# Scaling a gathered unit in three operations instead of one, in a deformable-convolution kernel

## The reference

```python
offset = conv3x3(x, w_off, b_off)              # two offsets for each of nine taps; C1 and C2 also a mask
py, px = row + tap_row + off_y, column + tap_column + off_x
for each of the four neighbours of (py, px):
    acc = acc + weight * valid * x[:, :, y_neighbour, x_neighbour]     # bilinear sample
out = einsum('bckhw,ock->bohw', acc * mask, w_dcn)
# batch norm, then relu (L0) or gelu (C1, C2); C2 also adds its block's input
```

## Time and profile before

| | |
|---|---|
| median of three runs | 10,226.54 us (10,207.91 to 10,236.34) |
| profiled execution, first to last instruction (span) | 7,289.1 us |
| profiled execution's own time | not shown apart; the runs' median less the span is 2,937.4 us |
| PE busy | 5,861.0 us, 80% |
| POOL busy | 5,125.5 us, 70% |
| DVE busy | 4,797.0 us, 66% |
| ACT busy | 2,151.4 us, 30% |
| gather issues on POOL | 4,896, 5,111.4 us, mean 1,044 ns |
| scale on DVE | 476 + 68, 647.2 + 92.3 us |

### The profile page before, as it was taken

The page is one execution under the profiler, slowest core; times in us unless marked ns, Lnnn a source line. Parts: engine busy times, 40 slices in busy tenths (PEclk is TensorE's granted clock), DMA queues, the critical chain, the costliest instruction groups (busy, mean ns, idle before and its releaser), DMA issues. The chain is left out here.

```text
span 7289.1 us, 123281 instructions
## 1 busy us (share of the span) xinstructions
PE 5861.0 (80%) x46325; PEld 4691.8 (64%) x46325; DVE 4797.0 (66%) x11223; ACT 2151.4 (30%) x3327; POOL 5125.5 (70%) x4909
## 2 busy tenths in 40 slices
PE   6985666664787887787887788879989998998996
PEld 6874555553666675576665565557767776776775
DVE  7875666664677775677775455546766766775665
ACT  1221212221222222222222222224444443443442
POOL 0007777777777776777776777767777777777776
PEclk9986777775888897788997788889989998998998
DMA  4322333333333332333332222223323333333332
GB/s 145 101 91 85 89 94 94 91 90 97 92 100 92 100 94 78 92 97 96 101 99 70 74 79 65 67 82 92 92 75 101 86 88 89 91 87 76 94 85 73
DMA packets 366225, 653.49 MB, mean 90 GB/s; under 512 B 113896, under 2 KB 272488, under 8 KB 357736
## 3 DMA queue, kind: packets, MB, share of 16 engines
q0 software_dynamic: 156672, 321.18, 17.2%
q1 hardware_dynamic: 209000, 324.67, 14.5%
HBM read 599.42 MB, written 46.07 MB: 89 GB/s over the span
## 5 line engine op out<-in xcount | busy, mean ns | idle before, releaser
L842 POOL DMA_INDIRECT G<-table,IDX x4896 | 5111.4, 1044 | 2117.4 <-issue 1987.3
L2098 DVE TENSOR_TENSOR ARENA<-ARENA 128x288 f32<-128x288 f32 x3744 | 1439.8, 449 | 243.2 <-PE RED L1064 218.9
L1064 PE MATMUL RED<-IDENT,ARENA 128*96 128x128 f32 x11232 | 1411.3, 288 | 211.7 <-DVE ARENA L2098 211.2
L1064 PEld LDWEIGHTS RED<-IDENT,ARENA 128*96 128x96 f32 x11232 | 1311.2, 134 | 296.2 <-issue 282.9
L1404 ACT ACTIVATE SAMP<-RED 96x384 f32<-96x384 f32 x1024 | 498.7, 487 | 3290.6 <-PE RED L1064 1317.7
L1931 DVE TENSOR_TENSOR G<-G,W 128x1152 f32<-128x1152 f32 x476 | 647.2, 1360 | 838.7 <-DMA G<-table,IDX 836.6
L1002 PE MATMUL OFFC<-PAD,ARENA 128*54 128x128 f32 (+1 forms) x10944 | 789.4, 306 | 27.2 <-ACT PAD L1310 15.4
L1209 PE MATMUL BTP<-PAD,ARENA 80*128 x2304 | 751.5, 449 | 71.0 <-DVE ARENA L1924 35.0
L1002 PEld LDWEIGHTS OFFC<-PAD,ARENA 128*54 128x54 f32 (+1 forms) x10944 | 706.7, 140 | 121.2 <-issue 98.4
L1049 PE MATMUL RED<-IDENT,SUM 128*96 128x128 f32 x672 | 164.1, 370 | 668.2 <-DVE SUM L1945 668.1
L1049 PEld LDWEIGHTS RED<-IDENT,SUM 128*96 128x96 f32 x672 | 83.6, 160 | 727.5 <-DVE SUM L1945 681.4
(11 more groups left out here) (209 smaller groups left out, 7031.6 us busy)
## 6 DMA issues: line engine op xcount, KB each, us to landing
ARENA<-wtab SPq DMA_DIRECT2D x208, 800.0 KB
G<-table,IDX POOLq DMA_INDIRECT x4896
ARENA<-xo SPq DMA_DIRECT2D x96, 720.0 KB
table<-TB SPq DMA_DIRECT2D x64, 384.0 KB, 2.6
X<-xo SPq DMA_DIRECT2D x64, 360.0 KB
X<-x SPq DMA_DIRECT2D x2, 3200.0 KB, 22.6
out<-X SPq DMA_DIRECT2D x20, 320.0 KB
wtab<-TB SPq DMA_DIRECT2D x16, 384.0 KB, 2.7
```

Of the source, the lines that this page charges most:

```text
L842: pool.indirect_dma_start(G[:, b, k, :], None, tables[seg.table], bass.IndirectOffsetOnAxis(ap=IDX[:, q, b * TAPS + k:b * TAPS + k + 1], a ...
L1064: last = nc.tensor.matmul(RED[b % 2][0:TPG * C, gr * 128:(gr + 1) * 128], PROD[gr][:, sft, :], IDENT[:, :], start=(sft == 0), stop=(sft == ...
L2098: last = nc.vector.tensor_tensor(out=PROD[gr][:, :, j * C:(j + 1) * C].rearrange("p (dy dx) c -> p dy dx c", dy=3), in0=win[:, gr:gr + 3, ...
```

## The change

`scale` for a unit becomes `scale_part`, called three times, once for each row of three taps: 3 x 4 x 32 = 384 values of a partition at a time. The first part waits for all nine gathers of the unit, the last one raises `z.scaled`. In the rounds `weight_rows` becomes `weight_row`, one tap at a time, with the same waits. The parts are laid between weightings: in a round after the second, third and fifth (scale stood after the third), in a half strip around them, the first part ahead of the weighting that used to precede scale. In a half strip `halve` and, for odd units, `sum_up` move back by one or two weightings. The steps of a gathered tile alone (`consume`) keep `scale`.

```diff
+                def scale_part(z, m, q, b, gr):
+                    if gr == 0:
+                        dve.wait_ge(z.gathered[b], 16 * TAPS * (m + 1))
+                    slots = G[:, b, TPG * gr:TPG * (gr + 1), :].rearrange("p k (s c) -> p (k s) c", s=CORNERS)
+                    k = b * TAPS + TPG * gr
+                    last = nc.vector.tensor_tensor(out=slots, in0=slots,
+                                                   in1=WEIGHTS[q][:, k:k + TPG, :].rearrange("p k s -> p (k s)").unsqueeze(2).to_broadcast([128, TPG * CORNERS, C]),
+                                                   op=ALU.mult)
+                    if gr == GROUPS - 1:
+                        last.then_inc(z.scaled, 1)
...
                     for b in range(UNITS):
-                        on.weight_rows(now, b, 0)
-                        on.scale(main, m, q, b)
+                        on.weight_row(now, b, 0)
+                        on.weight_row(now, b, 1)
+                        on.scale_part(main, m, q, b, 0)
+                        on.weight_row(now, b, 2)
+                        on.scale_part(main, m, q, b, 1)
...
-                        on.weight_rows(now, b, 1)
+                        on.weight_row(now, b, 3)
+                        on.weight_row(now, b, 4)
+                        on.scale_part(main, m, q, b, 2)
+                        on.weight_row(now, b, 5)
                         on.halve(main, m, b)
...
                     for im in range(2):
                         b = 2 * im
+                        on.scale_part(main, m, q, b, 0)
                         on.weight_half(half, im, 0)
-                        on.scale(main, m, q, b)
+                        on.scale_part(main, m, q, b, 1)
                         on.weight_half(half, im, 1)
+                        on.scale_part(main, m, q, b, 2)
+                        on.weight_half(half, im, 2)
                         on.halve(main, m, b)
-                        on.weight_half(half, im, 2)
                         on.weight_half(half, im, 3)
                         on.sum_up(main, m, b)
                         on.weight_half(half, im, 4)
-                        on.scale(main, m, q, b + 1)
+                        on.scale_part(main, m, q, b + 1, 0)
                         on.weight_half(half, im, 5)
+                        on.scale_part(main, m, q, b + 1, 1)
...
                         on.weight_half(half, im, 6)
+                        on.scale_part(main, m, q, b + 1, 2)
+                        on.weight_half(half, im, 7)
                         on.halve(main, m, b + 1)
-                        on.weight_half(half, im, 7)
+                        on.weight_half(half, im, 8)
                         on.sum_up(main, m, b + 1)
-                        on.weight_half(half, im, 8)
```

More of the change, by code:

```diff
@@ L1915, in first_strip, with weight_row @@
                     pass
-                def weight_rows(now, b, gr):
+                def weight_row(now, b, k):
+                    gr, j = k // TPG, k % TPG
                     si = now.s.first + now.k
[L1919 to L1926, removed]
+                    c = 36 * si + 9 * b + k
+                    if j == 0:
+                        dve.wait_ge(prod_used, WG_C2 + 12 * si + 3 * b + gr + 1)
+                    dve.wait_ge(taps, c + 1)
+                    nc.vector.tensor_tensor(
+                        out=PRODS[gr][:, :, j * C:(j + 1) * C], in0=TAP[c % TAPB][:, 0:TAPW].rearrange("p (w c) -> p w c", w=WY),
+                        in1=TY[now.k % 2][:, strip_unit(b) * TAPS + k, :].unsqueeze(2).to_broadcast([128, WY, C]), op=ALU.mult).then_inc(weighted, 1)
                 def scale(z, m, q, b):
@@ L1977, in round_ @@
                             on.place(*gprep)
-                        on.weight_rows(now, b, 2)
+                        on.weight_row(now, b, 6)
+                        on.weight_row(now, b, 7)
+                        on.weight_row(now, b, 8)
                         on.sum_up(main, m, b)
```

## The result

The changed kernel takes 10,305.08 us, the median of four runs (10,292.86 to 10,336.51), against 10,217.23 us before, also four (10,194.1 to 10,236.34): a ratio of 1.0092 with a 95% interval of 1.0066 to 1.0118. It is 0.9% slower, about 88 us. Forecast were 10,188 us and a range up to 10,238.

The account below looks back on a forecast made before the run. It took POOL's gather issues as the bound. 99 unphased units x 0.39 = 38.6 us, all other terms taken as 0, came off 10,226.5 for 10,188 us, range 10,142 to 10,238; the forecast's own chance was 0.52.

Parts of the forecast that it names:

- What bounds the kernel: Whole kernel: POOL's 4,896 gather issues at 1.25 us each set the pace, 6,120 of the profiled 7,289 us.
- The hold on POOL: Gather issues beginning inside a scale are held; parts hold less, gaining 0.39 us in each of 99 unphased units, 38.6 us.
- A part's duration: One 384-element part on DVE takes 550 ns, from a line through three measured shapes.
- DVE's added work: Three parts take 0.29 us more than one scale, 94 us over 320 units; taken as hidden, nothing counted.
- The moved wait: First part's wait for nine gathers now precedes one more weighting; bounds -26.6 to +21.6 us, taken as 0.
- The first: Rival 1: PE is the bound over the whole pair, building rounds' gain does not arrive; 20.7 us gained, 10,206; chance 0.20.
- The second: Rival 2: every second part holds the next gather issue, 0.23 us; all 240 units give +55 us, 10,282; chance 0.08.
- The third: Rival 3: parts on DVE wait for running gather issues, 0.71 us a unit more; +85 us, 10,312; chance 0.02.
- Rival 4: Nothing changes: phases rearrange, halve and sum take what scales give up; 10,226 us; chance 0.18.
- What would show it: Signs if right: POOL's mean issue about 8 ns below 1,044, DVE busy up some 90 us, gaps of 0.30 us staying.
- Rival 1: PE is the bound (10,206 us, chance 0.20); its mark: POOL waits for sums in building rounds without a shorter pair.

Follow-up runs that it names:

- e4: Kernel before with, in rounds only, three parts back to back where the one scale stood, after the third weighting: 1.0037 of before (1.0008 to 1.0066).
- e8: Kernel before with, in rounds only, the one whole scale moved ahead of the third weighting: 1.0074 of before (1.0042 to 1.0106).
- e2: Kernel before with the scale in three parts in the 32 half-strip steps only, rounds as before: 1.0003 of before (0.9973 to 1.0033).
- e5: Kernel before with, in rounds only, parts after the third, fourth and fifth weighting: 1.0392 of before (1.0353 to 1.0431).

## Why the prediction was wrong, by its steps

*What bounds the kernel* is the step that failed: "From the first gather on POOL runs through", and in the sum "2,937.4 us lie around the span (the execution's own time is not shown apart), taken as unchanged". A span 29% below the time was a warning that the execution profiled was another one; I booked the difference outside of the kernel. In the timed executions PE comes late, at places that its program does not name, and the rounds, as far as the waits show, are paced by PE and DVE waiting for each other. All that followed from POOL's pace had no bottleneck under it.

*The hold on POOL* was read rightly and is worth nothing. Issues became shorter by 27 ns in the mean (8 were forecast), and POOL spent it waiting for sums: 3,464.0 for 3,240.9 us.

*A part's duration*: 550 ns forecast, 548 the median. *DVE's added work*, taken as hidden with up to 94 us if its cover went, costs 0.08 to 0.66% for the 192 units of the rounds (e4), 38 us by the middle, where 192 x 0.29 = 56 would be all of it.

*The moved wait*, taken as 0 with +21.6 us as the upper bound: as a wait it is nothing, for the gathers have landed. As an order it is a term that the sum does not have, of either sign and by the middles at least as large as the splitting. A whole scale ahead of the third weighting costs 0.7% (e8), parts cost 0.6 to 0.7% in unit 1 or unit 2 and bring 0.65% in unit 3 alone. Both of its bounds, -26.6 and +0.47 x 46 us, came from pair 3's rounds, of the execution in which PE is not late, and the loss sits in the building rounds.

*The rivals.* Two had slower times near the result, 10,282 and 10,312, and neither is what happened. The first (PE is the bound, 10,206) is near in that POOL is not what sets the pace, but it still has a gain. The second (parts fall into POOL's beat) needs POOL's issues longer; they are shorter, in pair 3's rounds 972 ns for 1,017. The third (parts wait for running issues) needs parts well over 0.6 us; the longest of those shown is 606 ns. The Trainium skill's rule in SBUF — State Buffer, "Who interferes with whom", that whoever issues first keeps the shared pair, by which a part would be blocked until a running issue ends, stays without support here: 609 of the 960 parts begin inside a running issue, and the longest of these takes 586 ns. Rival 4 has the time of the half strips (1.0003), not the reason: in e2 the issues became shorter (1,000 ns for 1,008), halve and sum did not take it back; POOL waited for sums instead, 3,340.4 us for 3,240.9 (in e2's slowest execution).

*What would show it*: the marks named were POOL's issues down (seen), DVE's busy time up by some 90 us (4,790.4 to 4,819.4, 29 us, on the page, which counts overlapping operations once; the durations of parts and scales together are 95 us more), gaps of 0.30 us (seen), no issue under a part over 0.945 + 0.38 us (seen, 1,321 ns the longest). They came true and the time went the other way, because they watched an engine that waits. Rival 1's mark, POOL's waits for sums in building rounds, is there as well, and in the kernel before too: 833.3 us over the changed kernel's rounds of the pairs 0 to 2, 664.5 in the second profile of before.

What stays open is why PE comes late. The instruction stream, the packets moved and the busy times of DVE and ACT are those of the 7,289 us execution, while PE is busy 811 us longer; the late stretches fall on nearly the same convolutions from execution to execution (the one at 1,552.5 us takes 28.6 us in the second profile of before, 28.6 in e2, 28.6 and 28.1 in the two of the changed kernel, and 2.2 in the execution of 7,289 us), and no row names a cause. Half clock alone does not make them, since the 7,289 us execution has 2,030 us of it. POOL's gathers are a rival that no run here tests. The first gather issue stands at 553 us, and the first pause of PE over 0.3 us that ends by "issue" begins at 571 us, in the second profile of before as in the changed kernel. Take pauses less than 4 us apart as one late stretch: of those with over 5 us of pauses, 62 of 137 in the second profile of before and 49 of 113 in the changed kernel end 3 to 5 us after the ninth gather issue of a unit, where 11% of all instants lie; in e5 all 24 of DVE's copies at the hand-over that waited for "remote" start 2.5 to 2.7 us after such an issue. The engines' waits for each other could make such a pattern too, and the 7,289 us execution has the same gathers without lateness; so it stays a pointer.

So it is shown that POOL does not set the pace of the timed executions, that the loss is in the building rounds, that parts in unit 1 or unit 2 alone lose and in unit 3 alone gain, and that the lateness at the hand-over moves with the order of DVE's operations; it is not shown why one order draws it and another doesn't, nor that the lateness there is what the loss consists of.

## What to carry to other kernels

Before an argument is built on a profile, hold its span against the timed runs: all others here agreed to about 2 us, the one that lay 29% off was of another kind of execution, and its bottleneck was not the one that is timed. Where two engines hand work to each other in a tight order, apply an edit to one place of the loop body at a time, and then to several together; here one unit of four gained 0.65% by itself and two others lost as much, which the whole hid, and the gain was gone beside the others.

## What the runs showed of the hardware

One program has left a span of 7,289 us in one execution and of 10,200 us in another. In the longer ones PE has stretches in which matmuls without any semaphore start 0.7 us or a multiple of it apart (36 in 27.9 us for 2.17), in the hand-over shown DVE and ACT are released 11 and 13 us after the end that the trace models for the transposes that they wait for (7844.36 and 7842.10 to 7855.4), and nearly half of the time is at the half clock (4,880 of 10,200 us). The Trainium skill, Perfetto Trace Analysis, "Summary: the profiler window per engine type", lists TensorE's end as an estimate; the transpose that is shown to end at 7844.36, and for which DVE waits until 7855.43, agrees. A part that begins inside a gather issue is not held (609 of 960, the longest 586 ns), while an issue that begins inside a part or a scale is (up to 1.32 us under a part, for 0.945). Leaving out 324 transposes did not shorten the kernel by what can be told (0.998, 0.9953 to 1.0008).
